# A mixture-of-experts layer on Trainium2: experts two at a time, the four 48-row tail products in two row parts of the array

## The chip, the cores and the metric

The kernel runs on one core of a Trainium2 chip. The metric is device time in microseconds for one launch, the median over runs. The engines of the core are called PE (TensorE, matrix products), DVE (VectorE), ACT (ScalarE), POOL (GpSimd) and SP (SyncE, which here only issues DMAs); each has its own instruction stream and they meet at semaphores. All products are in float32. The profiler shows each float32 matrix product as two records, each with its own load of the stationary operand.

## The reference

An attention layer over 2048 tokens of 256 features (16 heads, a window of 32, 16 global tokens), then a mixture of 64 experts with six choices per token, and one shared expert for all tokens. The change touches the experts only:

```python
buf = zeros((E, C, D)).at[se, pos_c].add(x[st])          # C = 384 rows for each expert
g  = einsum('ecd,efd->ecf', buf, w_gate)                 # F = 176 hidden features
u  = einsum('ecd,efd->ecf', buf, w_up)
eo = einsum('ecf,edf->ecd', silu(g) * u, w_down)
y  = zeros_like(x).at[st].add(eo[se, pos_c] * sw)        # plus the shared expert
```

The hidden size of 176 is one full block of 128 features and a tail of 48 (`FT`). With these inputs no expert gets more than 256 tokens (`MAIN`, two blocks of 128), so the branch for larger counts does not run.

## The kernel before

The program has three stages. Attention, routing and most of the shared expert fill the first 277 us, token block by token block, and scatter each token's row to the rows of its experts in device memory (`expert_rows`). From 287 to 594 us the 64 experts run one after another. Then the two accumulators `acc_a` and `acc_b` are added into the output.

In the expert stage each engine runs a function `step(e)` for each expert, in the order in which its lines stand; nothing is reordered between the engines except through semaphores. For expert e:

- SP fetches the token rows into `XG` (L369, 272 KB) and the weights into `W1` (L362, 368 KB) and `W2` (L363, 128 KB, and L364, the 48-row tail, 48 KB). `XG`, `W1` and `W2` have four slots each. The loop of SP waits, for each expert m in turn, until PE has transposed the rows of m, then issues the rows of m+4; then it waits until the down product of m is done (`dn_done`) and issues the weights of m+4. The rows of m+4 thus stand in SP's stream behind the wait for the down product of m-1 and behind the weights of m+3.
- PE: `rows_t` (L679) transposes the 256 rows through PSUM bank 0 or 1, by the parity of e. `hidden` makes gate and up products of the 128 main features (L692, bank 2 or 3) and of the tail, 48 gate features in output rows 0 to 47 and 48 up features in rows 64 to 111 (L696, bank 4 or 7). `down` multiplies the hidden features by `W2` for both token blocks: the 128 main features (L707) and then the tail (L709), which is padded with zeros to 128 rows, so that both take a full pass of the array.
- The order on PE in `step(e)` is `hidden(e+1)`, `rows_t(e+2)`, `down(e)`: the products that ACT and DVE wait for lie one expert ahead of the down product that needs their result.
- ACT takes silu of the gate halves (L889, L891) and multiplies the down product by the token's weight into `YE` (L901, `weighted`). DVE multiplies silu by up into `HE` (L1176, L1179), copies the transposed rows out of PSUM (`XET`, L1167) and works out the weights and destinations of the tokens (`choices`, L1153 to L1158).
- POOL issues two indirect DMAs for each expert that add the rows of `YE` to `acc_a` or `acc_b` (L1303), even experts to one and odd ones to the other, each after the adds of two experts earlier have landed. The last expert goes to `acc_a` and waits for the expert before it.

The loop of SP, whose order matters below:

```python
hold(sp, et_done, i * UN + (j + 1))
hold(sp, idx_ready, i * UN + (j + 1))
expert_rows(i * UN + (j + UN), j, 0, n0)
hold(sp, dn_done, i * UN + (j + 1))
weights(i * UN + (j + UN), j)
```

Of the kernel before, what the change touches and what calls it, by code (L numbers as in the profile page):

```python
# [30 lines left out]
P = 128  # L31
# [70 lines left out]
def build(nc, x, glob, ln_s, ln_b, wq, wk, wv, wo, gate, w1, w2, shg, shu, shd, out):  # L102
# [4 lines left out]
    with ExitStack() as ctx:  # L107
# [111 lines left out]

        gkv_loaded, wq_loaded = sem("gkv_loaded"), sem("wq_loaded")  # L220
        ln_loaded, wog_loaded = sem("ln_loaded"), sem("wog_loaded")
        w2_clear = sem("w2_clear")
        ident_ready, mask_ready = sem("ident_ready"), sem("mask_ready")
        sh_loaded = sem("sh_loaded")
        init_done = sem("init_done")
# [101 lines left out]
        def has(e):  # L327
            return e.i is not None or 0 <= e.off < EX

        TAIL = (4, 7)  # L330


        NE = 3
# [12 lines left out]
        def _(sp):  # L346
# [14 lines left out]
            def weights(e, j):  # L361
                sp.dma_start(W1[:, j], w1[bass.ds(e, 1)].rearrange("e p c n -> p (e c) n")).then_inc(ew_loaded[j], 16)  # L362
                sp.dma_start(W2[:, j, 0, :], w2[bass.ds(e, 1), 0:P].rearrange("e p n -> p (e n)")).then_inc(ew_loaded[j], 16)  # L363
                sp.dma_start(W2[0:FT, j, 1, :], w2[bass.ds(e, 1), P:F].rearrange("e p n -> p (e n)")).then_inc(ew_loaded[j], 16)  # L364

            slots = rows.rearrange("(e t p) r -> e p t r", t=TPE, p=P)

# [3 lines left out]
            def step(s):  # L371
                a, e2 = s, s - LF
                if live(a):

                    sp.wait_ge(v_evac, a + 1)
                    if a >= UN:
                        sp.wait_ge(pv_done, RG * (a - UN + 1))
                    v = a % UN
                    sp.dma_start(VW[WIN:WK, v, 0], VS[0:BLK, a % UN]).then_inc(vw_loaded[v], 16)
                    sp.dma_start(VW[0:WK, v, 1], VS[BLK - WIN:P, a % UN]).then_inc(vw_loaded[v], 16)  # L380
                    if a > 0:
                        sp.dma_start(VW[0:WIN, v, 0], VS[P - WIN:P, (a - 1) % UN]).then_inc(vw_loaded[v], 16)
                if s == LF + 2:
                    sp.wait_ge(w2_clear, 1)
                    for j in range(UN):
                        weights(j, j)
                n = SG // P
                if e2 > 0 and e2 % n == 0 and e2 <= NL:
                    shared_out(e2 // n - 1)
# [31 lines left out]
            with sp.If(most > MAIN):  # L421
                with sp.Fori(0, EX // UN) as i:
                    for j in range(UN):
                        hold(sp, idx_ready, i * UN + (EX - UN + j + 1))
                        hold(sp, dn_done, i * UN + (EX - UN + j + 1))
                        expert_rows(i * UN + j, j, n0, TPE - n0)
                        weights(i * UN + j, j)
                sp.wait_ge(ew_loaded[0], 48)
            with sp.Else():
                sp.wait_ge(ew_loaded[0], 48)  # L430


            sp.wait_ge(y_stored[1], 16 * n0 * EX // UN)
# [7 lines left out]
        def _(pe):  # L441
# [227 lines left out]
            def experts(base, nt):  # L669
                n = nt * P  # L670

                def rows_t(e):

                    pe.wait_ge(xg_loaded[e.slot], e.turn(16, 16 + base * 16 // UN))
                    if base or not e.first(2):
                        pe.wait_ge(et_evac, e.times(1, base - 1))
                    for t in range(nt):
                        for d in range(DC):
                            mm = pe.transpose(PS[:, e.odd, d * MAIN + t * P:d * MAIN + (t + 1) * P],  # L679
                                              XG[:, e.slot, t, d * P:(d + 1) * P], ident[:, :])  # L680
                    mm.then_inc(et_done, 1)

                def hidden(e):
                    j, q = e.slot, e.odd
                    pe.wait_ge(ew_loaded[j], e.turn(48, 48 + base * 48 // UN))
                    pe.wait_ge(et_evac, e.times(1, base + 1))

                    if base or not e.first(2):
                        pe.wait_ge(h_ready, e.times(2, 2 * base - 2))
                    for u in range(2):  # L690
                        for d in range(DC):
                            mm = pe.matmul(PS[:, 2 + q, u * MAIN:u * MAIN + n], W1[:, j, d, u * P:(u + 1) * P],  # L692
                                           XET[:, q, d, 0:n], start=(d == 0), stop=(d == DC - 1))
                    mm.then_inc(gu_done, 1)
                    for d in range(DC):
                        mm = pe.matmul(PS[0:W1C - 2 * P, TAIL[q], 0:n], W1[:, j, d, 2 * P:W1C], XET[:, q, d, 0:n],  # L696
                                       start=(d == 0), stop=(d == DC - 1))
                    mm.then_inc(gt_done, 1)

                def down(e):  # L700
                    j, q = e.slot, e.odd

                    pe.wait_ge(h_ready, e.times(2, 2 * base + 2))
                    if base or not e.first(2):
                        pe.wait_ge(y_ready, e.times(1, base - 1))
                    for t in range(nt):
                        pe.matmul(PS[:, 5 + q, t * D:(t + 1) * D], HE[:, q, 0, t * P:(t + 1) * P], W2[:, j, 0, :],  # L707
                                  start=True, stop=False)
                        mm = pe.matmul(PS[:, 5 + q, t * D:(t + 1) * D], HE[:, q, 1, t * P:(t + 1) * P],  # L709
                                       W2[:, j, 1, :], start=False, stop=True)  # L710
                    mm.then_inc(dn_done, 1)

                def step(e):
                    if has(e + 1):
                        hidden(e + 1)
                    if has(e + 2):
                        rows_t(e + 2)
                    down(e)

                rows_t(Step(0))  # L720
                rows_t(Step(1))
                hidden(Step(0))
                in_flight(pe, step)

            experts(0, MAIN // P)
# [8 lines left out]
        def _(act):  # L734
# [145 lines left out]
            def experts(base, nt):  # L880
                n = nt * P

                def silus(e):
                    q = e.odd
                    act.wait_ge(gu_done, e.times(1, base + 1))

                    if base or not e.first(2):
                        act.wait_ge(h_ready, e.times(2, 2 * base - 2))
                    act.activation(SL[:, q, 0, 0:n], PS[:, 2 + q, 0:n], ACT.Silu).then_inc(silu_ready, 1)  # L889
                    act.wait_ge(gt_done, e.times(1, base + 1))  # L890
                    act.activation(SL[0:FT, q, 1, 0:n], PS[0:FT, TAIL[q], 0:n], ACT.Silu).then_inc(silu_ready, 1)  # L891

                def weighted(e):

                    act.wait_ge(dn_done, e.times(1, base + 1))
                    act.wait_ge(idx_ready, e.times(1, base + 1))

                    if base or not e.first(UN):
                        act.wait_ge(y_stored[e.slot], e.turn(16 * nt, base // UN * 32))
                    for t in range(nt):  # L900
                        i = act.mul(YE[:, e.slot, t, :], PS[:, 5 + e.odd, t * D:(t + 1) * D], wsel[:, e.slot, t:t + 1])  # L901
                    i.then_inc(y_ready, 1)

                def step(e):
                    if has(e + 1):
                        silus(e + 1)
                    weighted(e)

                silus(Step(0))
                in_flight(act, step)  # L910

            experts(0, MAIN // P)
# [8 lines left out]
        def _(dve):  # L921
# [27 lines left out]
            for q in range(4):  # L949
# [6 lines left out]
                if q == 0:  # L956
# [3 lines left out]
                    dve.memset(shg_s[:, :, FS:FSP], 0.0)  # L960
                    dve.memset(shu_s[:, :, FS:FSP], 0.0)
                    dve.memset(shd_s[FS - 2 * P:P, 2, :], 0.0)
                    dve.memset(HE[:, :, 1, :], 0.0)
                    dve.memset(W2[:, :, 1, :], 0.0).then_inc(w2_clear, 1)
            dve.wait_ge(w2_clear, 1)

            def split(v):
                return v.rearrange("p (c k) n -> p c k n", c=DC)

# [169 lines left out]
            def experts(base, nt, first):  # L1139
# [22 lines left out]
                def rows_t(e):  # L1162

                    dve.wait_ge(et_done, e.times(1, base + 1))
                    if base or not e.first(2):
                        dve.wait_ge(gt_done, e.times(1, base - 1))
                    dve.tensor_copy(XET[:, e.odd, :, 0:n],  # L1167
                                    PS[:, e.odd, :].rearrange("p (c n) -> p c n", c=DC)[:, :, 0:n]).then_inc(et_evac, 1)

                def products(e):  # L1170
                    q = e.odd
# [2 lines left out]
                    if base or not e.first(2):  # L1174
# [1 line left out]
                    dve.tensor_tensor(HE[:, q, 0, 0:n], SL[:, q, 0, 0:n], PS[:, 2 + q, MAIN:MAIN + n], ALU.mult)\  # L1176
                       .then_inc(h_ready, 1)
                    dve.wait_ge(silu_ready, e.times(2, 2 * base + 2))
                    dve.tensor_tensor(HE[0:FT, q, 1, 0:n], SL[0:FT, q, 1, 0:n], PS[64:64 + FT, TAIL[q], 0:n], ALU.mult)\  # L1179
                       .then_inc(h_ready, 1)  # L1180

                def step(e):
                    if has(e + 1):
                        products(e + 1)
                    if has(e + 2):
                        rows_t(e + 2)
                    if has(e + 1):
# [2 lines left out]
                rows_t(Step(0))  # L1190
                rows_t(Step(1))
                choices(Step(0))
                products(Step(0))
                in_flight(dve, step)

            experts(0, MAIN // P, 0)
# [181 lines left out]
```

## Time and profile before

| | us |
|---|---|
| median of 3 runs (629.52 to 632.45) | 631.92 |
| profiled execution, whole | 628.47 |
| its span | 626.7 |
| expert stage on PE, first transpose to last product | 286.65 to 593.5 |
| PE busy in the span | 556.0 (89%) |
| POOL, DVE, ACT busy in the span | 339.4, 340.8, 287.7 |

The profile's page divides the span into 40 slices of 15.7 us. A busy share is the share of a slice in which an engine executes; PE's is busy as long as any product is in flight, and the ends of the products are modelled. PEclk is the clock that PE was granted, in tenths of 2.4 GHz. The DMA share adds up how long the packets took over the 16 DMA engines; it can go over 1 where packets of two queues overlap on one engine.

### The profile page before, as it was taken

The numbers are of one execution on the slowest core, as the hardware profiler recorded it, in microseconds if no ns is written. First come the engines' busy times: TensorE is split into PE (matmuls) and PEld (weight loads), VectorE is DVE, ScalarE is ACT, GpSimd is POOL, SyncE is SP. The second block draws the span as 40 slices with busy tenths as digits, with TensorE's granted clock in tenths as the row PEclk, the third lists the DMA queues.
The fourth block names the chain that finished last, engine by engine and source line by source line (L and its number), as shares of the span: only waits on it lengthen the run. The fifth ranks groups of instructions, "written<-read, shape, count | busy, mean of one in ns | idle before, by whom it ended". The sixth has DMA issues, their size and how long they took to land.

```text
span 626.7 us, 14336 instructions
## 1 busy us (share of the span) xinstructions
PE 556.0 (89%) x4301; PEld 493.3 (79%) x4301; DVE 340.8 (54%) x1024; ACT 287.7 (46%) x847; POOL 339.4 (54%) x337
## 2 busy tenths in 40 slices
PE   2678999999998887998999999999999999999800
PEld 1578999999997876876888888888888888888700
DVE  7254788888877785843444444444444444444300
ACT  2597888877777782221333333333333333333300
POOL 4911255555544557740667666656666666666720
PEclk9998999999988887998999999999999999999965
DMA  8899969453222322243999999999999999999666
GB/s 275 332 392 406 369 250 361 122 187 112 78 77 69 107 75 97 89 125 106 207 233 237 228 222 238 237 221 228 239 229 230 239 230 224 232 239 221 94 168 134
DMA packets 78337, 127.81 MB, mean 204 GB/s; under 512 B 9969, under 2 KB 63025, under 8 KB 74929
## 3 DMA queue, kind: packets, MB, share of 16 engines
q0 software_dynamic: 26768, 59.00, 38.5%
q1 hardware_dynamic: 49760, 64.51, 34.4%
q10 hardware_dynamic: 1760, 3.69, 1.7%
q8 instruction: 27, 0.44, 0.3%
q14 instruction: 22, 0.17, 0.1%
HBM read 61.98 MB, written 66.06 MB: 204 GB/s over the span
## 4 chain that ended last, share of the span: by engine, by line
PE 79%; ACT 7%; DVE 6%; DMA 3%; issue 2%; POOL 1%; SPq 0%; POOLq 0%; DVEq 0%; ACTq 0%
PE PS L692 18%; PE PS L696 9%; PE PS L707 9%; PE PS L709 9%; PE PS L679 4%; PE PS L528 4%; PE PS L587 3%; ACT SM L769 3%; PE PS L547 3%; PE PS L553 3%; PE PS L611 3%; PE PS L467 2%; DMA acc_a<-YE,dest 2%; PE PS L497 2%; PE PS L626 2%
## 5 line engine op out<-in xcount | busy, mean ns | idle before, releaser
L1303 POOL DMA_INDIRECT acc_a<-YE,dest x66 | 102.6, 1554 | 86.5 <-issue 75.3
L692 PE MATMUL PS<-XET,W 128*128 128x256 f32 x512 | 122.7, 383 | 0.4 <-DVE XET L1167 0.4
L1290 POOL DMA_INDIRECT expert_rows<-XR,slot x96 | 94.9, 988 | 51.0 <-issue 28.7
L1303 POOL DMA_INDIRECT acc_b<-YE,dest x62 | 96.2, 1552 | 46.8 <-issue 43.2
L692 PEld LDWEIGHTS PS<-XET,W 128*128 128x128 f32 x512 | 98.3, 192 | 14.2 <-issue 0.6
L901 ACT ACTIVATE YE<-PS,wsel 128x256 f32<-128x256 f32 x128 | 53.8, 471 | 114.3 <-PE PS L709 114.3
L1176 DVE TENSOR_TENSOR HE<-SL,PS 128x256 f32<-128x256 f32 x64 | 27.0, 421 | 135.5 <-ACT SL L889 135.5
L707 PE MATMUL PS<-W,HE 128*128 128x256 f32 x256 | 76.3, 380 | 0.0
L709 PE MATMUL PS<-W,HE 128*128 128x256 f32 x256 | 76.1, 379 | 0.0
L769 ACT ACTIVATE SM<-SM,smax 128x112 f32<-128x112 f32 x256 | 75.1, 390 | 1.6 <-DVE smax L1014 1.6
L696 PE MATMUL PS<-XET,W 128*112 128x256 f32 x256 | 65.7, 379 | 0.0
L889 ACT ACTIVATE SL<-PS 128x256 f32<-128x256 f32 x64 | 24.6, 384 | 70.5 <-PE PS L692 70.5
L709 PEld LDWEIGHTS PS<-W,HE 128*128 128x128 f32 x256 | 48.6, 190 | 6.6
L696 PEld LDWEIGHTS PS<-XET,W 128*112 128x112 f32 x256 | 45.4, 177 | 9.2
L1268 POOL TENSOR_TENSOR rstd<-veps,power 128x1 f32<-128x1 f32 x16 | 9.1, 570 | 75.4 <-DVE veps L1033 75.4
L707 PEld LDWEIGHTS PS<-W,HE 128*128 128x128 f32 x256 | 43.8, 190 | 3.4
L1167 DVE COPY XET<-PS 128x512 f32<-128x512 f32 x64 | 44.2, 691 | 3.6 <-PE PS L679 1.7
L1000 DVE SCALAR_TENSOR_TENSOR SM<-PS,mask 128x448 f32<-128x448 f32 x64 | 35.4, 615 | 15.6 <-PE PS L467 15.6
L679 PE MATMUL PS<-ident,XG 128*128 128x128 f32 x256 | 38.3, 273 | 1.9 <-issue 1.9
L679 PEld LDWEIGHTS PS<-ident,XG 128*128 128x128 f32 x256 | 31.9, 141 | 9.4 <-issue 2.3
L1179 DVE TENSOR_TENSOR HE<-SL,PS 48x256 f32<-48x256 f32 x64 | 27.1, 423 | 22.1 <-ACT SL L891 22.1
L528 PE MATMUL PS<-ident,SM 128*112 128x128 f32 x256 | 37.0, 292 | 0.0
(150 smaller groups left out, 900.4 us busy)
## 6 DMA issues: line engine op xcount, KB each, us to landing
expert_rows<-zero POOLq DMA_DIRECT2D x24, 1088.0 KB, 20.4
W<-in_w SPq DMA_DIRECT2D x64, 368.0 KB, 3.9
XG<-expert_rows SPq DMA_DIRECT2D x64, 272.0 KB, 3.8
W<-in_w SPq DMA_DIRECT2D x64, 128.0 KB, 3.8
W<-in_w SPq DMA_DIRECT2D x64, 48.0 KB, 4.1
acc_a<-zero ACTq DMA_DIRECT2D x1, 2432.0 KB, 15.2
X<-in_x SPq DMA_DIRECT2D x4, 512.0 KB, 7.6
acc_b<-X SPq DMA_DIRECT2D x4, 512.0 KB
```

The costliest lines, as they stand in the source:

```text
L528: mm = pe.transpose(PT_ps[:, n, k, :], SM[:, b2 % 2, NJ * n + k, :], ident[:, :])
L679: mm = pe.transpose(PS[:, e.odd, d * MAIN + t * P:d * MAIN + (t + 1) * P], XG[:, e.slot, t, d * P:(d + 1) * P], ident[:, :])
L692: mm = pe.matmul(PS[:, 2 + q, u * MAIN:u * MAIN + n], W1[:, j, d, u * P:(u + 1) * P], XET[:, q, d, 0:n], start=(d == 0), stop=(d == DC - 1))
L696: mm = pe.matmul(PS[0:W1C - 2 * P, TAIL[q], 0:n], W1[:, j, d, 2 * P:W1C], XET[:, q, d, 0:n], start=(d == 0), stop=(d == DC - 1))
L707: pe.matmul(PS[:, 5 + q, t * D:(t + 1) * D], HE[:, q, 0, t * P:(t + 1) * P], W2[:, j, 0, :], start=True, stop=False)
L709: mm = pe.matmul(PS[:, 5 + q, t * D:(t + 1) * D], HE[:, q, 1, t * P:(t + 1) * P], W2[:, j, 1, :], start=False, stop=True)
L769: i = act.activation(SM[:, b % 2, h], SM[:, b % 2, h], ACT.Exp, bias=smax[:, b % 2, h:h + 1])
L901: i = act.mul(YE[:, e.slot, t, :], PS[:, 5 + e.odd, t * D:(t + 1) * D], wsel[:, e.slot, t:t + 1])
L1000: dve.scalar_tensor_tensor(out=sm, in0=sp_, scalar=SM_SCALE, in1=mk, op0=ALU.mult, op1=ALU.add).then_inc(s_read, 1)
L1167: dve.tensor_copy(XET[:, e.odd, :, 0:n], PS[:, e.odd, :].rearrange("p (c n) -> p c n", c=DC)[:, :, 0:n]).then_inc(et_evac, 1)
L1290: pool.indirect_dma_start(rows, bass.IndirectOffsetOnAxis(ap=slot[:, d2 % UN, k:k + 1], axis=0), XR[:, d2 % UN, :], None, bounds_check=EX ...
L1303: pool.indirect_dma_start(target, bass.IndirectOffsetOnAxis(ap=dest[:, e.slot, t:t + 1], axis=0), YE[:, e.slot, t, :], None, bounds_check= ...
```

## The change

Experts are taken in pairs (e, e+1), e even.

- On PE `step(e)` is now `hidden(e)`, `rows_t(e+2)`, and after the odd expert of a pair come the main down products of both experts (`down_main`) and then the tail products of both (`down_tail`). In one pair PE does: hidden(e), rows(e+2), hidden(e+1), rows(e+3), main(e), main(e+1), tail(e), tail(e+1).
- The tail product reads 48 rows, not 128. The tail of token block 0 stands in SBUF rows 0 to 47, that of block 1 in rows 64 to 111, both in `HE` and in `W2`; the four products of a pair write the four banks 1, 5, 6 and 7 (`DOWN`), half a bank each.
- For that, SP loads the 48-row tail of `W2` twice, once to each place (one DMA of 48 KB more for each expert), and DVE makes the tail of `HE` in two instructions of 48 x 128 where it was one of 48 x 256. The zero fill of `HE` and `W2` and its semaphore are gone.
- To free two banks, the transposed rows all go through bank 0, and the hidden tail always through bank 4. Each has a wait of its own: the rows for the copy of the last rows, the tail for DVE's product of the last tail.
- ACT does `silus(e)` in each step, and `weighted` of both experts after the odd one. DVE's step is moved in the same way (`products(e)`).

```diff
-        w2_clear = sem("w2_clear")
...
         def has(e):
...
-        TAIL = (4, 7)
+        TAIL, DOWN = 4, ((1, 5), (6, 7))
...
             def weights(e, j):
...
-                sp.dma_start(W2[0:FT, j, 1, :], w2[bass.ds(e, 1), P:F].rearrange("e p n -> p (e n)")).then_inc(ew_loaded[j], 16)
+                for t in range(2):
+                    sp.dma_start(W2[64 * t:64 * t + FT, j, 1, :], w2[bass.ds(e, 1), P:F].rearrange("e p n -> p (e n)"))\
+                      .then_inc(ew_loaded[j], 16)
...
-                    sp.wait_ge(w2_clear, 1)
                     for j in range(UN):
...
-                sp.wait_ge(ew_loaded[0], 48)
+                sp.wait_ge(ew_loaded[0], 64)
...
-                sp.wait_ge(ew_loaded[0], 48)
+                sp.wait_ge(ew_loaded[0], 64)
...
                 def rows_t(e):
...
-                    if base or not e.first(2):
-                        pe.wait_ge(et_evac, e.times(1, base - 1))
+                    if base or not e.first():
+                        pe.wait_ge(et_evac, e.times(1, base))
                     for t in range(nt):
                         for d in range(DC):
-                            mm = pe.transpose(PS[:, e.odd, d * MAIN + t * P:d * MAIN + (t + 1) * P],
+                            mm = pe.transpose(PS[:, 0, d * MAIN + t * P:d * MAIN + (t + 1) * P],
...
                 def hidden(e):
...
-                    pe.wait_ge(ew_loaded[j], e.turn(48, 48 + base * 48 // UN))
+                    pe.wait_ge(ew_loaded[j], e.turn(64, 64 + base * 64 // UN))
...
+                    if base or not e.first():
+                        pe.wait_ge(h_ready, e.times(2, 2 * base))
                     for d in range(DC):
-                        mm = pe.matmul(PS[0:W1C - 2 * P, TAIL[q], 0:n], W1[:, j, d, 2 * P:W1C], XET[:, q, d, 0:n],
+                        mm = pe.matmul(PS[0:W1C - 2 * P, TAIL, 0:n], W1[:, j, d, 2 * P:W1C], XET[:, q, d, 0:n],
...
-                def down(e):
+                def down_main(e):
...
-                    pe.wait_ge(h_ready, e.times(2, 2 * base + 2))
+                    pe.wait_ge(h_ready, e.times(2, 2 * base + 1))
...
                     for t in range(nt):
-                        pe.matmul(PS[:, 5 + q, t * D:(t + 1) * D], HE[:, q, 0, t * P:(t + 1) * P], W2[:, j, 0, :],
+                        pe.matmul(PS[:, DOWN[q][t], 0:D], HE[:, q, 0, t * P:(t + 1) * P], W2[:, j, 0, :],
...
-                        mm = pe.matmul(PS[:, 5 + q, t * D:(t + 1) * D], HE[:, q, 1, t * P:(t + 1) * P],
-                                       W2[:, j, 1, :], start=False, stop=True)
...
+                def down_tail(e):
+                    j, q = e.slot, e.odd
+                    pe.wait_ge(h_ready, e.times(2, 2 * base + 2))
+                    for t in range(nt):
+                        r = slice(64 * t, 64 * t + FT)
+                        mm = pe.matmul(PS[:, DOWN[q][t], 0:D], HE[r, q, 1, t * P:(t + 1) * P], W2[r, j, 1, :],
+                                       start=False, stop=True)
...
                 def step(e):
-                    if has(e + 1):
-                        hidden(e + 1)
+                    hidden(e)
...
-                    down(e)
+                    if e.odd:
+                        down_main(e - 1)
+                        down_main(e)
+                        down_tail(e - 1)
+                        down_tail(e)
...
-                hidden(Step(0))
...
-                    act.activation(SL[0:FT, q, 1, 0:n], PS[0:FT, TAIL[q], 0:n], ACT.Silu).then_inc(silu_ready, 1)
+                    act.activation(SL[0:FT, q, 1, 0:n], PS[0:FT, TAIL, 0:n], ACT.Silu).then_inc(silu_ready, 1)
...
                 def weighted(e):
...
                     for t in range(nt):
-                        i = act.mul(YE[:, e.slot, t, :], PS[:, 5 + e.odd, t * D:(t + 1) * D], wsel[:, e.slot, t:t + 1])
+                        i = act.mul(YE[:, e.slot, t, :], PS[:, DOWN[e.odd][t], 0:D], wsel[:, e.slot, t:t + 1])
...
                 def step(e):
-                    if has(e + 1):
-                        silus(e + 1)
-                    weighted(e)
...
-                silus(Step(0))
+                    silus(e)
+                    if e.odd:
+                        weighted(e - 1)
+                        weighted(e)
...
-                    dve.memset(HE[:, :, 1, :], 0.0)
-                    dve.memset(W2[:, :, 1, :], 0.0).then_inc(w2_clear, 1)
-            dve.wait_ge(w2_clear, 1)
...
             def split(v):
...
-                                    PS[:, e.odd, :].rearrange("p (c n) -> p c n", c=DC)[:, :, 0:n]).then_inc(et_evac, 1)
+                                    PS[:, 0, :].rearrange("p (c n) -> p c n", c=DC)[:, :, 0:n]).then_inc(et_evac, 1)
...
                 def products(e):
...
-                    dve.tensor_tensor(HE[0:FT, q, 1, 0:n], SL[0:FT, q, 1, 0:n], PS[64:64 + FT, TAIL[q], 0:n], ALU.mult)\
-                       .then_inc(h_ready, 1)
+                    for t in range(nt):
+                        c = slice(t * P, (t + 1) * P)
+                        i = dve.tensor_tensor(HE[64 * t:64 * t + FT, q, 1, c], SL[0:FT, q, 1, c],
+                                              PS[64:64 + FT, TAIL, c], ALU.mult)
+                    i.then_inc(h_ready, 1)
...
                 def step(e):
-                    if has(e + 1):
-                        products(e + 1)
+                    products(e)
...
-                products(Step(0))
```

## Rows read from the trace of the kernel before

**Rows 1.** Windows, expert stage: us, PE, PEld, DVE, ACT, POOL busy, clock, DMA share, GB/s.

```profile
320.00:586.00 266.00, 266.00 (x1344) 231.48 (x1343) 120.76 (x392) 89.70 (x224) 173.96 (x113) 1.00 0.99 228
```

**Rows 2.** Chain that ended last, one expert: start us, us, what, records.

```profile
316.42 1.73 PE PS L692 x8
...
319.01 0.44 PE PS L679 x4
319.44 0.43 PE PS L707 x2
...
321.17 0.86 PE PS L692 x4
```

**Rows 3.** Timeline of PE: column parts, 32-row parts, full array; start us, us, records.

```profile
207.33 0.51 PE L611 MATMUL PS<-VW,PT 112*64 112x17 f32 x12
207.76 1.70 PE L467 MATMUL PS<-KW,QT 32*128 32x112 f32 x32
...
209.39 0.33 PE L480 MATMUL PS<-ident,XR 128*128 128x128 f32 x1
```

**Rows 4.** Lines of PE by form, 320 to 586 us: busy us, mean ns of one.

```profile
L679 PE MATMUL PS<-ident,XG 128*128 128x128 f32 x224 | 33.6, 273 | 0.0
```

**Rows 5.** Timeline of all engines, end of one down product to the rows' DMA.

```profile
453.74 0.59 PE L709 MATMUL PS<-W,HE 128*128 128x256 f32 x2
...
454.37 0.84 ACT L901 ACTIVATE YE<-PS,wsel 128x256 f32<-128x256 f32 x2 [1.79 <-PE PS L709]
454.56 0.34 SPq L362 DMA_DIRECT2D W<-in_w  x1
...
455.61 0.33 SPq L364 DMA_DIRECT2D W<-in_w  x1
...
456.25 1.55 POOL L1303 DMA_INDIRECT acc_b<-YE,dest  x1 [1.19 <-issue]
456.34 0.38 SPq L369 DMA_DIRECT2D XG<-expert_rows  x1
...
458.11 1.55 POOL L1303 DMA_INDIRECT acc_b<-YE,dest  x1 [0.30 <-issue]
```

**Rows 6.** DMA, row loads of seven experts, 451 to 480 us: us from issue to landing.

```profile
XG<-expert_rows SPq DMA_DIRECT2D x1, 272.0 KB, 4.2
...
XG<-expert_rows SPq DMA_DIRECT2D x1, 272.0 KB, 4.4
...
XG<-expert_rows SPq DMA_DIRECT2D x1, 272.0 KB, 3.1
...
XG<-expert_rows SPq DMA_DIRECT2D x1, 272.0 KB, 3.8
```

**Rows 7.** DMA, 400 to 500 us: packets, MB, share of 16 engines; the adds' landing.

```profile
q1 hardware_dynamic: 13117, 17.59, 59.6%
q0 software_dynamic: 6078, 5.54, 40.9%
...
acc_b<-YE,dest POOLq DMA_INDIRECT x22, 5.1
```

**Rows 8.** Windows of PE: us, PE busy, clock, DMA share, GB/s.

```profile
464.50:465.00 0.50, 0.50 (x4) 1.00 0.36 51
```

**Rows 9.** Timeline of the end: last adds, copies of the accumulators.

```profile
594.74 0.57 SPq L435 DMA_DIRECT2D out<-acc_b  x1
595.32 1.55 POOL L1303 DMA_INDIRECT acc_a<-YE,dest  x1 [0.31 <-issue]
604.81 1.55 POOL L1303 DMA_INDIRECT acc_a<-YE,dest  x1 [7.95 <-DMA acc_a<-YE,dest]
...
611.76 1.02 POOL L1339 DMA_DIRECT2D out<-acc_a  x1 [3.54 <-issue]
```

**Rows 10.** Timeline of DVE: zero fill at the start, first copy of rows.

```profile
10.17 0.91 DVE L964 MEMSET W<- 128x1024 f32 x1 [0.16 <-issue]
...
287.34 1.29 DVE L1167 COPY XET<-PS 128x512 f32<-128x512 f32 x2 [1.71 <-PE PS L679]
```

## The prediction

> **What bounds the kernel now.** I read the stages first, by windows. From 320 to 586 us PE is busy without a gap, at the full granted clock (2.4 GHz), while DVE, ACT and POOL are busy 45%, 34% and 65% of the time; the DMA share is 0.99, which needs a second look [rows 1]. The chain that ended last lies on PE for that whole stage and repeats for each expert [rows 2]: 12 records of the hidden products from 316.42 to 319.01 (2.59 us), 4 transposes (0.44), 8 records of the down product at 0.43 for two (1.73). The next expert starts at 321.17, so an expert takes 4.755 us and a pair 9.51 (the pieces add up to 4.75). One record of 256 columns is a step of 0.216 us. No wait is on this path: the stage is bound by PE's stream.
>
> **What is taken out.** Of 40 steps of 0.216 in a pair, 8 are tail records of the down product. In two row parts they take 4 steps' time if the parts run beside each other, 0.86 us less. Does float32 work run so? L467 is a product on 32-row parts, four of them, 8 records in each. The 32 records take 1.70 us [rows 3]; a whole-array product of 128 columns steps at 0.109 (4 in 0.44, [rows 2]), so one behind the other they would need 31 x 0.109 + 0.27 = 3.6 us. So parts do overlap. 64-row parts with 256 columns are not in this trace; I take the full overlap (0.86) since nothing but the width differs, with none at all as the other end.
>
> The Trainium skill (TensorE: Matmul & The Clock Gate, Part 3, The mechanism) says that a weight load overlaps a running product only where it goes to another row group. With that rule each part here would wait out its product (0.38, from 0.59 for two records less a step) at each of its four records, and the tails would cost some 1.5 us and not 0.86, which takes the whole gain. The trace speaks against it: 8 records of L467 in one part would last over 8 x 0.27 = 2.2 us, and all 32 are done in 1.70.
>
> **What is added on PE: two changes of the array's division in each pair.** Into 32-row parts: L611 ends at 207.84 and L467 starts at 207.76, 0.08 before that end. Out of them: L467 ends at 209.46 and L480 starts at 209.39, 0.07 before [rows 3]. In a steady stream a record of 256 columns starts 0.379 - 0.216 = 0.163 before the end of the one ahead, where 0.379 is 0.59 less a step [rows 5], so a change costs 0.163 - 0.07 = 0.09; the first record behind it is also longer (0.33 against 0.273, [rows 3, 4]), 0.06. That is 0.15 out and, with the longer first record inside the parts, 0.18 in: 0.33 for a pair. A pair on PE alone is then 2 x (2.59 + 0.44) + 1.73 + 0.86 + 0.33 = 8.98 us. Against 9.51 this is 0.53 less, and 17.0 over 32 pairs.
>
> **What moves in SP's queue.** This is the term that I think decides. The rows of expert e+3 are issued behind the wait for the down product of e-2 and the weights of e+2. Before, PE wants these rows over two experts later. Now PE finishes e-2 and e-1 together at the end of a pair and wants the rows of e+3 in the middle of the very next one. With t = 0 at the end of e-2's product:
> - PE: tail(e-1) ends two steps later (0.43), the next record starts 0.07 before that (0.36); the longer first record 0.06, hidden(e) 2.59, rows(e+2) 0.44, hidden(e+1) 2.59: it comes to rows(e+3) at 6.04.
> - SP before: the product ends at 454.33, W1 is issued at 454.56 (+0.23), the last weight DMA at 455.61 (0.525 apart), the rows at 456.34 (+0.73) [rows 5]. They land 4.2, 4.4, 3.5, 3.1, 3.8, 4.1, 3.8 us after issue for seven experts in turn, mean 3.84 [rows 6]. So they would be there at 0.23 + 1.05 + 0.73 + 3.84 = 5.85.
> - The second copy of the W2 tail stands ahead of them. If the rows wait for SP's issue it adds 0.52; if they wait for the DMA engines it adds its own transfer: the hardware queue used 59.6% of 100 us for 17.59 MB [rows 7], so 49 KB take 0.16. I take the middle, since the issue and the queue both are near: 6.19.
> - The stall, with 0.05 for the wait and 0.06 for a first record from standstill, is 0.26 at the mean landing. It can't be negative, and with the seven landings one by one (0.62, 0.82, 0, 0, 0.22, 0.52, 0.22) it is 0.34. It comes in 30 of the 32 pairs (rows 0 to 3 are loaded ahead): 10.2 us given back. Bounds: landings of 3.1 give 0; all of 4.4 with the full 0.52 give 1.0, which is 30 us.
>
> **The other added waits.** PE's hidden tail of e+1 waits for DVE's product of the tail of e: there are 2.2 us between (rows and main products) for silu, product and now one instruction more, against under 1 us before; hidden. Rows through one bank: rows(e+3) need the copy of rows(e+2), 0.65 us each [rows 10], with 2.59 us of hidden(e+1) between; hidden. At the start, before any product, that copy is bare: +0.3 us once. ACT does both weighted products in the 1.73 us in which PE makes the next main products (2 x 0.84, [rows 5]); then silu comes in time. Behind the weighted product, POOL gets two experts at once. For one it needs 2 x 1.55 + 0.30 and at most 1.19 of waits [rows 5], 4.6; two are 9.2, against 9.3 for a pair: close, but the 1.19 holds waiting for ACT. DVE's `choices` waits for the adds of four experts earlier, issued some 5 us behind the pair's start and landing 5.1 later [rows 7], about 1 us before DVE comes there. More SP issues (10 in a pair, 5.5 us) fit. The zero fill, 0.91 and a smaller one, lies early on DVE [rows 10] while the chain runs over POOL and ACT: 0.
>
> **The end.** PE ends at 593.5. The copy of `acc_b` is issued at 594.74, and the second add of expert 62, issued at 595.32, gets caught in it: expert 63 starts at 604.81; the last copy is issued at 611.76 [rows 9], 18.2 behind PE. Now the adds of 61 come later (POOL serves 60 and 61 late), the copy goes out some 2 us later and the adds of 62 go out some 1.3 us later, perhaps just ahead of it. If they escape, up to 2.7 less; if not, 2.1 more. I take -1.0.
>
> **The sum**, against the profiled execution of 628.47: -17.0 + 10.2 + 0.3 - 1.0 = -7.5, 621.0. The median of the runs is 631.92, 3.45 above the profiled one, so the same difference gives **624.4**.
>
> **Rivals.**
> - A, the forecast: rows late by 0.1 to 0.5 us a pair, 614 to 629 with the end. 0.43.
> - B, the rows come in time: DMA queues are empty when a pair's burst begins, so landings may shrink to 3.1. Then 631.9 - 17.0 + 0.3 - 1.0 = 614.2; with a good end 612.5. For it: [rows 8], where the DMA share falls to 0.36 between bursts. Against it: landings hold at 3.8. 0.22.
> - C, slower: the rows of e+3 set the pair. One mechanism: the pair lasts from the end of e-2's product to its rows (2.35 + landing + issue) and on through rows, main and tail to the end of e's product. It equals 9.51 where the stall is 0.53, a landing of 4.1 us at the middle value. At 4.4, which one of seven reached, the stall is 0.82 (1.0 with the full issue) and 30 pairs give back 25 to 30: 639 to 645. For it: two experts' weights and rows now go out in one burst of 5.5 us, with the adds across it. Against it: the burst's second half stands behind these rows. 0.15.
> - D, it doesn't do what it says: 48-row products are taken as full ones, or 64-row parts don't overlap. Then the pair is 8.98 + 0.86 = 9.84 and 32 x 0.33 = 10.6 come on top: 642. For it: no 48- or 64-row operation is in the trace. Against it: L467 and L611 divide the array by the rows and columns of their operands alone. 0.08.
> - E, the DMA engines are the bound. Shares of 59.6% and 40.9% make 1.005 [rows 7], 4.78 us of every expert; with 0.16 more it is 4.94, a pair 9.88, +11.8 us: 643. Against it: the share counts overlaps (it goes over 1), landing times stay level, and there are dips [rows 8]. A saturation that merely holds the old pace would end near no change. 0.12.
>
> **How the numbers follow.** A measurement of this kernel can tell about 0.5% (3.2 us) from no change. A lies over that gain in 0.35 of its 0.43, within it in 0.08; B is faster; C is slower in 0.12 and the same in 0.03; D slower; E half and half. Faster 0.57, same 0.17, slower 0.26. The range from 613 to 640 holds A, nearly all of B and the near part of C; D, most of E and the far end of C are left out.
>
> **What would show it.** In the profile after: the tail records of 48 rows in pairs some 10 ns apart, 8 in about 0.86 plus 0.2 (D otherwise); PE idle ahead of the transposes in every second expert, released by the DMA of `XG` (none in B, over 0.5 in C); the first record behind each change longer by 0.06 to 0.09; landings of the rows near 4; PE's clock still full; pairs 9.3 us apart in the chain. PE idle for `W`, or landings of all loads above 5, would speak for E. I am wrong as a whole if the tails show no overlap, if the landings move by more than 0.3 us from 3.84, or if PE waits on ACT or DVE in each pair.

## The result and the profile after

| | us | ratio to the kernel before (95% interval) |
|---|---|---|
| changed kernel, median of 4 runs (643.26 to 655.29) | 646.21 | 1.022 (1.018 to 1.027) |
| the same file again, 4 runs (635.73 to 644.99) | 641.06 | 1.018 (1.010 to 1.025) |
| kernel before, beside the first and the second of these | 632.18, 629.83 | |
| forecast | 624.4 (613 to 640) | |

The change makes the kernel slower by about 2%, and the time is outside the range. The first profile of the changed kernel was taken in its longest run, so the lines below are those of its second one (span 636.8 us), if nothing else is said.

The windows of the expert stage (us, then busy time of PE, PEld, DVE, ACT and POOL, granted clock, DMA share, GB/s) answer to [rows 1]:

```profile
320.00:585.00 265.00, 248.45 (x1287) 197.61 (x1286) 127.77 (x431) 82.12 (x214) 166.94 (x108) 0.99 0.95 232
```

PE, busy without a gap before, now has 16.6 us without work in 265, and does 1287 records there where it did 1344 in 266. The lines of PE in that stretch (records, busy us, mean ns of one, then idle time before them and what ended it) name the place:

```profile
L692 PE MATMUL PS<-XET,W 128*128 128x256 f32 x425 | 103.4, 386 | 0.0
L710 PE MATMUL PS<-W,HE 128*128 128x256 f32 x216 | 54.3, 397 | 0.0
L679 PE MATMUL PS<-ident,XG 128*128 128x128 f32 x216 | 33.3, 277 | 16.5 <-DMA XG<-expert_rows 16.5
L718 PE MATMUL PS<-W,HE 48*128 48x256 f32 x216 | 30.6, 402 | 0.0
```

Nearly all of the idle time (16.5 of 16.6) stands ahead of the transposes (L679), and the DMA of the token rows ends it. The chain that ended last, which was PE alone in [rows 2], shows one such pair (start us, us, what; a line `...` stands for lines left out):

```profile
404.89 0.86 PE PS L692 x4
405.76 0.86 PE PS L699 x4
406.62 0.44 PE PS L679 x4
407.06 1.73 PE PS L692 x8
408.79 0.86 PE PS L699 x4
...
409.68 0.65 PE PS L679 x4
410.33 1.73 PE PS L710 x8
412.06 0.66 PE PS L718 x4
...
412.94 0.35 SPq L361
...
414.43 0.37 SPq L364
...
415.20 5.37 DMA XG<-expert_rows
...
420.70 0.65 PE PS L679 x4
```

The down product of the even expert ends, SP issues W1 at 412.94 and four DMAs later, at 415.20, the rows; they land at 420.57, and PE, which had come to them 1.9 us earlier, goes on at 420.70. The next lines are the timeline of PE, SP and POOL in that pair:

```profile
411.99 1.14 PE L718 MATMUL PS<-W,HE 48*128 48x256 f32 x8
413.06 1.99 PE L692 MATMUL PS<-XET,W 128*128 128x256 f32 x8
414.90 1.55 POOL L1311 DMA_INDIRECT acc_a<-YE,dest  x1 [2.39 <-ACT YE L912]
415.20 0.40 SPq L370 DMA_DIRECT2D XG<-expert_rows  x1
...
416.76 1.55 POOL L1311 DMA_INDIRECT acc_a<-YE,dest  x1 [0.30 <-issue]
417.92 1.03 PE L699 MATMUL PS<-XET,W 128*112 128x256 f32 x4
418.62 1.55 POOL L1311 DMA_INDIRECT acc_b<-YE,dest  x1 [0.30 <-issue]
420.48 1.55 POOL L1311 DMA_INDIRECT acc_b<-YE,dest  x1 [0.31 <-issue]
```

Read off the first tail record of each pair, the 30 full pairs are from 9.04 to 13.85 us apart, 12 of them by 9.05 or less; before it was 9.51 for every pair. PE's part of the change does what it should; more than it gave is lost in the other pairs. A pair that waits is longer than 9.05 by its idle time and some 0.2 us more (in the first profile one with 1.73 idle takes 10.99). Most of that is the 0.16 by which a record in the unbroken stream starts ahead of the end of the one before it: idle time is counted from that end. From first transpose to last product the stage takes 316.5 us, against 306.9 before; in the first profile it takes 326.0.

### The profile page after: what moved, and what is told of

Read it like the earlier page. It is cut to its first block, busy times and chain, and to the rows that moved or that the text cites. A ratio compares the mean times of both kernels' runs of the same rounds, so it can differ in the third digit from the quotient of the medians.

```text
span 653.5 us, 14523 instructions
## 1 busy us (share of the span) xinstructions
PE 556.4 (85%) x4301; PEld 471.2 (72%) x4301; DVE 352.4 (54%) x1086; ACT 284.0 (43%) x847; POOL 339.4 (52%) x337
## 4 chain that ended last, share of the span: by engine, by line
PE 60%; DMA 16%; ACT 7%; DVE 5%; SPq 5%; issue 4%; POOL 1%; ACTq 0%; POOLq 0%; DVEq 0%
DMA XG<-expert_rows 13%; PE PS L710 9%; PE PS L692 9%; PE PS L718 4%; PE PS L699 4%; PE PS L587 4%; PE PS L679 4%; PE PS L528 4%; PE PS L547 3%; ACT SM L780 3%; PE PS L611 3%; PE PS L553 3%; PE PS L467 2%; SPq L364 2%; DMA acc_a<-YE,dest 2%
## 5 line engine op out<-in xcount | busy, mean ns | idle before, releaser
L692 PE MATMUL PS<-XET,W 128*128 128x256 f32 x512 | 126.0, 389 | 0.0
L692 PEld LDWEIGHTS PS<-XET,W 128*128 128x128 f32 x512 | 93.3, 192 | 20.6 <-issue 10.3
L912 ACT ACTIVATE YE<-PS,wsel 128x256 f32<-128x256 f32 x128 | 50.3, 476 | 111.1 <-PE PS L718 111.1
L679 PE MATMUL PS<-ident,XG 128*128 128x128 f32 x256 | 40.6, 283 | 28.4 <-DMA XG<-expert_rows 25.4
L710 PE MATMUL PS<-W,HE 128*128 128x256 f32 x256 | 63.4, 392 | 0.0
L679 PEld LDWEIGHTS PS<-ident,XG 128*128 128x128 f32 x256 | 31.1, 143 | 41.5 <-issue 36.4
L710 PEld LDWEIGHTS PS<-W,HE 128*128 128x128 f32 x256 | 48.1, 198 | 5.7
L1188 DVE TENSOR_TENSOR HE<-SL,PS 48x128 f32<-48x128 f32 x128 | 37.2, 291 | 21.8 <-ACT SL L902 20.9
L789 ACT COPY PT<-PS 112x512 f32<-112x512 f32 x64 | 34.7, 589 | 5.9 <-PE PS L528 5.7
L718 PE MATMUL PS<-W,HE 48*128 48x256 f32 x256 | 36.3, 402 | 0.0
```

The source lines that it names most:

```text
L679: mm = pe.transpose(PS[:, 0, d * MAIN + t * P:d * MAIN + (t + 1) * P], XG[:, e.slot, t, d * P:(d + 1) * P], ident[:, :])
L710: pe.matmul(PS[:, DOWN[q][t], 0:D], HE[:, q, 0, t * P:(t + 1) * P], W2[:, j, 0, :], start=True, stop=False)
L718: mm = pe.matmul(PS[:, DOWN[q][t], 0:D], HE[r, q, 1, t * P:(t + 1) * P], W2[r, j, 1, :], start=False, stop=True)
L912: i = act.mul(YE[:, e.slot, t, :], PS[:, DOWN[e.odd][t], 0:D], wsel[:, e.slot, t:t + 1])
L1188: i = dve.tensor_tensor(HE[64 * t:64 * t + FT, q, 1, c], SL[0:FT, q, 1, c], PS[64:64 + FT, TAIL, c], ALU.mult)
```

## The experiments

Two theories stood against each other. **R**: the rows of expert e+3 come late, since they stand in SP's queue behind the down product of e-2 and the weights of e+2. **S**: the DMA engines are saturated, and 48 KB more for each expert lengthen everything.

### The changed kernel again

> The changed kernel, unaltered, beside the others on one chip. Both theories expect its first result again: 641 to 650 us, 1.7 to 2.7% over the kernel before. In its profile, unstalled pairs of experts 9.05 us apart, the others 10 to 13, the difference being PE idle ahead of the transposes of every second expert.

Measured: 641.06 us, ratio 1.018 (1.010 to 1.025). Its runs spread over 9 us, where the kernels below without a stall spread over 2 to 6.

### Rows first in SP's loop

The diffs from here on are shortened; two lines of a loop may stand for several of the kernel.

```diff
-for j in range(UN):
-    hold(et_done), hold(idx_ready); expert_rows(j + UN)
-    hold(dn_done); weights(j + UN)
+for j0 in range(0, UN, 2):
+    for j in (j0, j0 + 1):
+        hold(et_done), hold(idx_ready); expert_rows(j + UN)
+    for j in (j0, j0 + 1):
+        hold(dn_done); weights(j + UN)
```

> The changed kernel with one edit in SP's loop: for each pair of experts the two row loads are issued first (each behind the same two waits as before) and the four plus four weight loads behind the waits for the two down products; so no row load stands behind a down product of the pair just ended. Bytes and number of DMAs are unchanged. Theory R (the rows of expert e+3 come late because of their place in SP's queue): the idle time goes, pairs are 9.05 us apart, and against 9.51 in the kernel before that is 0.46 x 32 = 14.7 us less: 614 to 621 us. Theory S (the DMA engines are saturated, with 48 KB more for each expert): the order does not matter, stalls turn up elsewhere (weights, or rows again), 635 us or more.

> The changed kernel with the row loads first in SP's loop, once more with more rounds, beside the three others on one chip: 616 to 620 us, 1.7 to 2.3% under the kernel before.

Measured: 618.07 us, ratio 0.980 (0.977 to 0.984), and with more rounds 618.30, 0.983 (0.979 to 0.987). The windows and the chain of this kernel (some of its line numbers are one higher than above):

```profile
320.00:585.00 265.00, 263.26 (x1396) 213.69 (x1394) 136.62 (x463) 91.09 (x236) 182.03 (x118) 1.00 1.02 245
...
420.24 1.06 PE PS L719 x8
421.30 1.92 PE PS L693 x8
423.23 0.86 PE PS L700 x4
424.09 0.44 PE PS L680 x4
424.53 1.73 PE PS L693 x8
426.26 0.86 PE PS L700 x4
427.12 0.44 PE PS L680 x4
427.56 1.73 PE PS L711 x8
429.29 1.06 PE PS L719 x8
```

The chain is PE alone again, and each pair takes 9.05 us (420.24 to 429.29); the stage takes 292.3 us. The same bytes in the same DMAs as in the changed kernel (232 GB/s) now pass at 245 GB/s; the kernel before had 228 at a share of 0.99 that looked full. S is out, and with it rival E: 24.2 of the stage's 316.5 us (33.7 of the 326.0 in the first profile) were the place of the row loads in SP's queue. The rows' landing is no shorter here (median 4.6 us between 400 and 500 us); it only has a pair's time to hide in. This kernel beats both others.

### One expert at a time, with the row parts

The order of steps on PE, ACT and DVE is that of the kernel before; the down product of each expert is followed by its own tails in two row parts.

```diff
-    hidden(e)
+    hidden(e + 1)
     rows_t(e + 2)
-    if e.odd: down_main(e - 1); down_main(e); down_tail(e - 1); down_tail(e)
+    down_main(e)
+    down_tail(e)
```

> The changed kernel with the old order of steps on PE, ACT and DVE: one expert at a time, its products one expert ahead, and behind its two main down products its two 48-row tails in the two row parts. The second copy of the W2 tail is still loaded. Theory R: the rows' issue is as early as in the kernel before, no stall; each expert saves two of four tail steps (0.43 us) and pays for two changes of the array's division, which cost 0.41 in the changed kernel's unstalled pair (9.05 less 2 x 3.03, 1.73 and 0.86), so about nothing is left: 627 to 634 us. Theory S: the added bytes alone make the stage longer, 637 to 645 us.

Measured: 630.99 us, ratio 1.002 (1.000 to 1.005). Its chain:

```profile
420.28 1.92 PE PS L692 x8
422.20 0.86 PE PS L699 x4
423.07 0.44 PE PS L679 x4
423.51 0.86 PE PS L710 x4
424.37 0.63 PE PS L718 x4
425.00 1.95 PE PS L692 x8
```

An expert takes 4.72 us where it took 4.755: the two changes of the array's division eat what two saved steps give (0.43). Experts in twos are what makes the row parts pay. The second copy of the tail is loaded here too, without a stall, which speaks against S once more.

### Pairs with full-array tails, and the same with rows first

The tails run over 128 rows, padded with zeros, and the W2 tail is loaded once; order, banks and waits are those of the changed kernel.

```diff
-    r = slice(64 * t, 64 * t + FT)
-    mm = pe.matmul(PS[:, DOWN[q][t], 0:D], HE[r, q, 1, ...], W2[r, j, 1, :], ...)
+    mm = pe.matmul(PS[:, DOWN[q][t], 0:D], HE[:, q, 1, ...], W2[:, j, 1, :], ...)
```

> Pairs without the row parts: the changed kernel's order, banks and waits, but the tails are full passes of the array (padded with zeros to 128 rows, filled once at the start) and the tail of W2 is loaded once, as before the change. Theory R: PE alone would need 9.51 us for a pair, as before; it comes to the rows of e+3 0.43 us later than in the changed kernel and they are issued 0.5 earlier, so landings up to 4.4 us after issue cost nothing; at the landings that the changed kernel shows there (2.7 to 6.1, mean 4.2) some 0.3 to 0.6 us a pair remain: 636 to 652 us, slower than before, with PE idle ahead of the same transposes. If landings fall back to the 3.8 of the kernel before: 630 to 635. Theory S: no added bytes, so 632.

> Pairs with full-array tails and one copy of the W2 tail, and with the row loads first in SP's loop: neither the row parts nor the late rows. What is left of the change is its order, banks and waits. If these cost nothing of their own (as I hold), PE streams at 9.51 us a pair: 628 to 634 us, the kernel before within 0.5%; against rows_first (618) that gives the worth of the row parts by themselves, 0.46 us a pair. If the pairing has a cost beyond the late rows (ACT's two weighted products, POOL's four adds in a row, single banks): 636 or more.

Measured: 639.26 us, ratio 1.011 (1.005 to 1.017), for the pairs alone; with the rows first 630.07, 1.000 (0.997 to 1.004). The lines of the first, between 320 and 585 us, show idle time at the same place:

```profile
L679 PE MATMUL PS<-ident,XG 128*128 128x128 f32 x220 | 33.8, 276 | 5.0 <-DMA XG<-expert_rows 4.5
```

Its pairs take 9.51 to 11.05 us, and all 9.51 or 9.52 with the rows first; the stage takes 317.1 and 307.3 us, against 306.9 in the kernel before. So the pairing by itself costs 1.1%, all of it through the rows, and its banks, its bursts on ACT and POOL and its other waits cost nothing that can be measured once the rows are in time. Between this last kernel (630.1) and the one with rows first and row parts (618.1 and 618.3) lies the worth of the row parts, 12 us. In the stage it is 15.0 (307.3 less 292.3), as 0.46 us a pair make 14.7. What follows the stage is the same within 0.4 us; what differs is the start of the stage, at 291.0 and 289.4 in the two profiles with row parts and at 285.8 in this one. That start varies from run to run (292.4 and 285.8 in the two profiles of the changed kernel), so the stage tells the worth of the parts better than the whole time does.

### One copy of the W2 tail in the loop

The copy in rows 64 to 111 stays that of the first four experts, so the tails of token block 1 use stale weights.

```diff
-    for t in range(2):
+    for t in range(1):        # 2 for the first four experts
         sp.dma_start(W2[64 * t:64 * t + FT, j, 1, :], ...)
```

> The changed kernel, but inside the loop the 48-row tail of W2 is loaded to rows 0 to 47 only; the copy in rows 64 to 111 stays that of the first four experts (so the tails of token block 1 use stale weights from the fifth expert on). It measures the term of the second copy: its issue (0.52 us ahead of the rows) and its transfer (0.16). Both theories expect less stall; by the sum, 0.16 to 0.52 us less in each of the pairs that stall (10 or more of 30 stall fully, the others partly): 5 to 16 us under the changed kernel's 641 to 646, so 627 to 638. If the second copy is what lengthens the landings beyond its size: under 625.

Measured: 630.29 us, ratio 1.002 (0.998 to 1.005). Its stage takes 309.1 us, 7.4 less than in the second profile of the changed kernel, 0.25 for each of the 30 pairs, and 16.9 less than in the first. From W1 to the rows it is 1.74 us in the mean, where it was 2.24. The landings of the rows of e+3 are no shorter: between 3.4 and 5.4 us, mean 4.4. So the second copy costs the time of its issue ahead of the rows (0.50), and doesn't lengthen the landing.

### Fewer adds

Three kernels tell why the landings grew: one with only the first of the two adds of each expert, one with the adds of even experts only, one with those of odd experts only. In each, half of the routed rows are left out of the sum.

```diff
-                for t in range(nt):
+                for t in range(1):          # half the adds
                     pool.indirect_dma_start(target, ...)
```

```diff
+                if e.odd == 1:              # even experts only; == 0 for the other
+                    pool.sem_inc(y_stored[e.slot], 16)    # twice
+                else:
                     added(e, ...)
```

> The changed kernel with only the first of the two adds of each expert (half of the rows are left out of the sum, and so half of POOL's instructions and of the adds' DMA traffic). It tells why the rows of e+3 land later than 3.84 us after issue (2.7 to 6.1, mean 4.3 in the changed kernel, short and long ones taking turns). Theory A (the adds of the last pair, four in a row behind a pair's end, get in the way of these rows): the landings of these rows fall to 2.7 to 3.5, the idle time ahead of the transposes goes, 612 to 620 us. Theory B (the rows queue behind the pair's own five hardware DMAs, the second tail copy among them): they stay above 4 and the time stays above 630.

> The changed kernel in which POOL issues the adds of even experts only (the odd experts' half of the routed sum is left out). In the changed kernel four adds follow a pair's end: two of the even expert, out from about 1.8 us after the first weight DMA of the new pair on and thus across the rows of e+3, then two of the odd one, which go on until the next pair's start. Theory A1 (the adds of the same pair, in flight beside the rows, lengthen their landing): mean landing of the rows of e+3 stays above 4 us and the stalls stay, 630 us or more. Theory A2 (the late adds of the pair before hold up the weights ahead of the rows): landing falls to 3.0 to 3.4, stage at 9.05 us a pair, 612 to 620 us.

> The same with the adds of odd experts only. They go out as soon as the odd expert's products are weighted, some 0.9 us later than those of the even one in the changed kernel, two and not four. A1: they are in flight beside the rows too, landing 3.7 to 4.5, 625 us or more. A2: nothing is left over from the pair before either, landing 3.0 to 3.4, 612 to 620 us. If both kernels are quick, it takes all four adds (more than the half of them) to delay the rows.

Measured: 616.33 us, 0.976 (0.970 to 0.981); 616.18 us, 0.976 (0.969 to 0.983); 611.43 us, 0.969 (0.962 to 0.977). The stage takes 292.8, 294.6 and 292.5 us, as with the rows first. (The whole times hold a shorter end as well: the last copy is issued 14.8, 12.6 and 11.7 us behind PE's last product, 19.4 in the changed kernel and the one with rows first, so the stage is the number to compare.) The landings of the rows of e+3, expert by expert, are 2.6 to 3.8 us (mean 2.98), 2.8 to 4.1 (3.12) and 2.7 to 3.6 (3.01). Theory B, the pair's own hardware DMAs, is out: they are all there. In the kernel with even adds the two adds go out as in the changed one, one ahead of the rows and one behind (W1 at 440.49, the rows at 442.68):

```profile
442.23 1.55 POOL L1311 DMA_INDIRECT acc_a<-YE,dest  x1 [5.54 <-ACT YE L912]
442.68 0.40 SPq L370 DMA_DIRECT2D XG<-expert_rows  x1
...
444.09 1.55 POOL L1311 DMA_INDIRECT acc_a<-YE,dest  x1 [0.30 <-issue]
```

Two adds in flight beside the rows thus don't delay them, and A1 is out. What is gone in all three is the second half of the four adds, which in the changed kernel run up to the start of the next pair. That these are in the way (A2) fits all three, but the last expectation named another reading, that any more than two adds would do it, and no run here separates the two. The first profile of the changed kernel leans to A2. Of 29 pairs, 16 have the last add of the pair before issued at most 2.3 us ahead of W1, and their rows land in 5.1 us in the mean; 12 have it at least 3.3 us ahead, and theirs land in 3.3. Four adds a pair go out in both groups, the first of them 0.4 us ahead of the rows. (In the second profile, where 22 pairs can be read: 4.75 for the first group, and 3.0 for the seven others.) But a late W1 also follows a pair that waited, in which every queue had longer to empty, and in the kernel with one copy there is no such difference (means of 4.39 and 4.45 with the last add under and over 2.3 us ahead). So it is shown that the adds lengthen the landing, and not by which way.

## Why the prediction was wrong

**What bounds the kernel before** held: PE's stream, and no wait on it. The DMA share near 1 was no bound.

**What is taken out and added on PE** held. The tails' 8 records take 1.14 us from first start to last end (411.99 above). In series, whether on the full array or in one part, 8 records of 0.38 at steps of 0.216 would take 7 x 0.216 + 0.38 = 1.89. They start in twos 7 ns apart, and these twos follow one another at 0.32, 0.216 and 0.216 us, while a record lasts 0.38. The rule of the Trainium skill (TensorE: Matmul & The Clock Gate, Part 3, The mechanism), that a weight load overlaps a running product only where it goes to another row group, would give an estimated 4 x 0.38 = 1.5 at the least; the trace doesn't agree, and the measurement decides. The two changes of division cost 9.05 - 8.65 = 0.40 for a pair, 0.33 was forecast: the tails take 1.06 to the next record (0.86 and 0.20) and the next eight 1.92 where they take 1.73. An unstalled pair is 9.05, 8.98 was forecast, so 32 pairs gain 14.7 us and not 17.0.

**What moves in SP's queue** was the right mechanism, named as rival C with its place, and it was mis-sized: 10.2 us given back in the sum, 24.2 measured (316.5 less the 292.3 of the same kernel with the rows first), and 33.7 in the first profile. The decision point was forecast at a landing of 4.1 us. Two parts of the term were off.
- The issue. I took the middle (0.34) between the second copy's transfer and its issue. W1 to rows is 2.26 us (412.94 to 415.20), 1.78 before, so the issue counts in full (0.48 to 0.50).
- The landing. I took the seven landings of [rows 6] over unchanged, mean 3.84. In the first profile of the changed kernel the 30 landings of the rows of e+3 run from 2.7 to 6.3, mean 4.2, and long and short ones take turns (5.3, 3.2, 5.7, 3.9, 5.1, 3.1, 5.5); those that can be read in the second profile run from 2.7 to 6.5. The move of the mean by 0.4 is more than the 0.3 that the prediction named as a sign of being wrong. A stall can't be negative, so the spread costs more than the mean tells. With the sum's own steps and the measured issue and pair, a landing up to about 3.45 is free; the 30 landings give 28.5 us of stall in all, the seven of before would give 13. That run's 30 pairs are 32 us over 9.05 in all, and 3.4 of it is the lower clock (below). So of that run's 28.5 us, about 3 more than the sum had are the issue and 15 the landings.

The step that failed is the landing in the stall term: the seven landings of the kernel before, mean 3.84, were taken over as they were, with no bound above 4.4. They come from a kernel in which two adds follow each expert; in the changed one four follow each pair, and the landings reach 6.3. Rival C did name "the adds across it", but no price was put on them, and the rival was set aside with "against it: the burst's second half stands behind these rows", which looks at the rows' own queue alone. The four adds in a row were weighed only against POOL's time, where they fit. With half of the adds the same rows land in 3.0 and the stall is gone.

**The other added waits** cost nothing, as forecast (pairs with full-array tails and the rows first: 1.000), and the start cost 0.4 (that kernel's stage, 307.3, against 306.9), where 0.3 was forecast.

**The end** went the other way: the copy of `acc_b` goes out as the second add of expert 62 does, and that is caught again.

```profile
604.65 0.57 SPq L435 DMA_DIRECT2D out<-acc_b  x1
605.38 1.55 POOL L1311 DMA_INDIRECT acc_a<-YE,dest  x1 [0.30 <-issue]
614.97 1.55 POOL L1311 DMA_INDIRECT acc_a<-YE,dest  x1 [8.04 <-DMA acc_a<-YE,dest]
616.82 1.55 POOL L1311 DMA_INDIRECT acc_a<-YE,dest  x1 [0.30 <-issue]
621.75 1.02 POOL L1347 DMA_DIRECT2D out<-acc_a  x1 [3.37 <-issue]
```

PE ends at 602.3; the last copy is 19.4 behind it, against 18.2 in [rows 9]: +1.2 for a forecast of -1.0.

So of the 16.7 us between the forecast and the second measurement, 14.0 are the stall (24.2 for 10.2); the price of the two changes of division (2.3) and the end (2.2) went the same way, and the rest, under 2 us the other way, is within what runs of one kernel differ by.

**The rivals.** D (the parts don't overlap) and E (DMA bound) are out by the kernel with the rows first. B's time, 614.2, is 4 us under what the kernel reaches with the rows first. C's price of 639 to 645 holds one of the two measurements of the changed kernel, 641, and the other, 646, is 1 us above; its chance of 0.15 was too small, since its point of decision, a landing of 4.1, lay only some 0.3 us above the mean of before, and the measured growth of 0.4 goes beyond it. C's way to that time was in part another one: single stalls of up to 2.9 us between pairs with none, and not one of 0.8 to 1.0 in each.

## What to carry to other kernels

When products are grouped so that results come in pairs, list for every DMA the event that it is queued behind and the moment when it is wanted, both in the new order: a load that had an expert's time to spare can lose all of it though no line that issues it was touched, and the cure here was its place in the queue (23 us here, 641 to 618, from the order of two calls). Where the spare time left is within a few tenths of a landing time, don't carry the landing over from the old kernel; its spread, and what the other queues will carry at that moment, set the cost. Two changes of the array's division cost as much as two steps of 256 columns, so in this kernel row parts paid only where more than that was saved between them.

## What the runs showed of the hardware

Float32 products of 48 rows in two 64-row parts of the array overlap in full (8 records in 1.14 us, 1.89 in series), at 0.20 us a change of division, and the cost lies partly in the products behind the change (1.92 for eight in place of 1.73).

The landing time of a 272 KB load from device memory to SBUF depends on what the adds on another queue do: in the three kernels with half of them it was 3.0 to 3.1 us in the mean (2.6 to 4.1), with all of them 4.2 (2.7 to 6.3), behind the same weight loads.

A stall can cost more than its idle time. In the first profile of the changed kernel PE stood idle for 2.4 us ahead of 477.09, and then was granted half the clock for 3.4 us (us, PE busy, clock, DMA share, GB/s):

```profile
474.40:477.00 2.60, 0.31 (x2) 0.99 1.13 283
477.00:480.40 3.40, 3.31 (x10) 0.50 0.84 158
480.40:484.00 3.60, 3.60 (x20) 1.00 0.29 67
```

That pair took 13.2 us. In the windows above PE does ten records in the 3.4 us at half the clock, and twenty in the 3.6 us after it. Such a stretch came twice within the expert stage in each of the two profiles of the changed kernel, each behind one of its longest stalls (2.2 to 2.9 us idle), and in none of the kernels with the rows first or with fewer adds once the stage was under way. Not every long stall brought one: the longest of the first profile, 2.7 us, did not.
